# Four groups' weights held in a mixture of experts with capacity, and tokens gathered in three bf16 parts with one one-hot per pair of groups

## The reference, cut to what matters

```python
scores = jax.nn.softmax(x @ gate_w.T, axis=-1)
topk_w, topk_i = jax.lax.top_k(scores, K)
# pos: the place of a token in its expert's queue, in order of tokens
valid = pos < CAP
slot = jnp.where(valid, pos, CAP)
buf = jnp.zeros((E, CAP + 1, H), x.dtype).at[flat_i, slot].set(x[token_ids])
g = jnp.einsum('ech,ehi->eci', buf, w_gate)
u = jnp.einsum('ech,ehi->eci', buf, w_up)
y = jnp.einsum('eci,eih->ech', jax.nn.silu(g) * u, w_down)
out_slots = y[flat_i, slot] * (flat_w * valid)[:, None]
moe = out_slots.reshape(T, K, H).sum(axis=1)
shared = jax.nn.silu(x @ sw_gate) * (x @ sw_up) @ sw_down
```

## Time and profile before

| | us |
|---|---|
| median of 3 runs | 1891.27 |
| fastest, slowest of them | 1882.26, 1895.61 |
| profiled execution, its own time | 1897.17 |
| span of that execution | 1895.4 |

### The profile page before, as it was taken

One profiled execution on the slowest core, in us unless ns is written; L12 is line 12 of the kernel. 1 busy time (PEld: TensorE's weight loads), 2 busy tenths in 40 slices (PEclk: granted clock), 3 DMA queues, 4 the chain that ended last, 5 costly groups with the idle time before them and its releaser, 6 DMA issues.

```text
span 1895.4 us, 34583 instructions
## 1 busy us (share of the span) xinstructions
PE 1684.1 (89%) x10911; PEld 1349.1 (71%) x10912; DVE 1336.7 (71%) x2830; ACT 1020.7 (54%) x2200; POOL 659.1 (35%) x604
## 2 busy tenths in 40 slices
PE   3877999899999899989999998988799999988986
PEld 1224888677777888867777786756588888887664
DVE  7996777788884677777877656643788888656543
ACT  4665543578774554267777633111688888633111
POOL 1664410366661230046655422000455555321000
PEclk8998999899999899989999998988799999999989
DMA  1000210000000121000000012887011000012985
GB/s 62 0 1 25 84 51 1 15 20 19 19 6 35 42 76 43 1 23 18 24 20 11 15 47 62 257 228 203 26 31 33 25 25 17 30 44 87 255 222 148
DMA packets 34885, 111.36 MB, mean 59 GB/s; under 512 B 4992, under 2 KB 18544, under 8 KB 27888
## 3 DMA queue, kind: packets, MB, share of 16 engines
q1 hardware_dynamic: 34800, 110.26, 20.3%
HBM read 109.19 MB, written 1.05 MB: 58 GB/s over the span
## 4 chain that ended last, share of the span: by engine, by line
PE 57%; DVE 18%; DMA 10%; ACT 8%; issue 6%; ACTq 0%; DVEq 0%; POOL 0%; SPq 0%; POOLq 0%
DMA wgu<-in_w_gu 10%; PE banks L1033 7%; PE banks L1009 4%; PE banks L583 3%; PE banks L585 3%; PE banks L584 3%; PE banks L988 3%; PE banks L989 2%; PE banks L990 2%; ACT prob L1217 2%; PE banks L940 2%; PE banks L1047 2%; PE banks L942 2%; PE banks L941 2%; PE banks L1048 2%
## 5 line engine op out<-in xcount | busy, mean ns | idle before, releaser
L1457 POOL TENSOR_TENSOR xn<-xn 128x512 f32<-128x512 f32 x132 | 171.5, 1299 | 254.7 <-DVE xn L1341 254.7
L1443 POOL TENSOR_SCALAR prob<-prob,recip 128x256 f32<-128x256 f32 (+2 forms) x256 | 228.3, 907 | 68.1 <-DVE recip L1325 68.1
L1217 ACT ACTIVATE prob<-banks,peak 128x256 f32<-128x256 f32 (+3 forms) x384 | 190.3, 501 | 109.9 <-DVE peak L1316 99.9
L1033 PE MATMUL banks<-pt,v 128*128 128x256 f32 (+3 forms) x768 | 203.1, 407 | 7.2 <-ACT pt L1152 7.2
L1033 PEld LDWEIGHTS banks<-pt,v 128*128 128x128 f32 x768 | 143.6, 189 | 73.7 <-issue 32.9
L1316 DVE TENSOR_REDUCE peak<-banks 128x1 f32<-128x256 f32 (+3 forms) x384 | 161.3, 448 | 16.4 <-PE banks L992 15.4
L988 PE MATMUL banks<-k_hi,q_hi 128*128 128x256 f32 (+2 forms) x384 | 151.3, 394 | 24.1 <-DVE k_lo L1332 23.8
L1428 POOL TENSOR_TENSOR wq_lo<-wq,wq_hi 128x256 fp32r<-128x256 f32 x48 | 35.9, 748 | 343.2 <-ACT wq_hi L1167 343.2
L1009 PE MATMUL banks<-ident,prob 128*128 128x128 f32 x864 | 139.4, 277 | 3.2 <-DVE pt L1150 3.2
L1341 DVE TENSOR_TENSOR xn<-xn,ropes 128x512 f32<-128x512 f32 x138 | 122.4, 887 | 0.0
L681 POOL TENSOR_TENSOR w_parts<-raw,w_parts 128x768 fp32r<-128x768 f32 x36 | 67.3, 1870 | 157.3 <-ACT w_parts L637 157.3
(11 more groups left out here) (249 smaller groups left out, 5058.5 us busy)
## 6 DMA issues: line engine op xcount, KB each, us to landing
wgu<-in_w_gu SPq DMA_DIRECT2D x32, 1408.0 KB, 15.3
wd<-in_w_d SPq DMA_DIRECT2D x32, 704.0 KB
raw<-in_w SPq DMA_DIRECT2D x36, 384.0 KB, 3.1
wkv<-in_mha_kv SPq DMA_DIRECT2D x16, 256.0 KB, 2.7
wq<-in_mqa_q SPq DMA_DIRECT2D x16, 128.0 KB, 2.0
wo<-in_mqa_o SPq DMA_DIRECT2D x16, 128.0 KB, 2.1
wq<-in_gqa_q SPq DMA_DIRECT2D x16, 128.0 KB, 2.0
wo<-in_gqa_o SPq DMA_DIRECT2D x16, 128.0 KB, 2.1
```

Source lines behind the costliest of these rows:

```text
L1033: last = pe.matmul(o_bank[:, x * P:to], v[:, s, x, at:at + P], pt[:, s, x, first:first + to - x * P], start=(j == 0), stop=(j == NQ - 1))
L1217: last = act.activation(prob[:, s, cols[t]:cols[t] + n], s_bank[gi][:, psum_col[t]:psum_col[t] + n], ACT.Exp, bias=peak[:, s, t:t + 1], ac ...
L1443: last = pool.tensor_scalar(part, part, recip[:, s, t:t + 1], None, ALU.mult)
L1457: pool.tensor_tensor(cosed_at(i, m, r), cosed_at(i, m, r), swap[:, r % 2, :], ALU.add) \
```

## The change

- `wgu` and `wd` get four buffers each instead of two, so that the transfer for group n waits for group n-4. The loop's body is four groups long instead of two. The transfers of groups 0 and 1 are issued right behind those of the shared weights, before SP waits for `opened`; groups 2 and 3 behind it.
- To make room, `x_hi` and `x_lo` (fp32r) become `x_parts`, three parts in bf16. ACT makes the first, DVE takes it from `xn` in place, ACT makes the second, DVE the third. `gather` takes 48 matmuls instead of 32.
- `picks` and the buffer `pick` are gone. `pair` is bf16, has two buffers, and `weigh` and `spread` read the half of it that belongs to their group (`one_hot`). `spread` so waits for the pair (`paired`) where it waited for the group's own one-hot (`picked`).
- Other tiles move to other places in SBUF.

```diff
-    BODY = 2
+    BODY = 4
+    HALF = BODY // 2
...
+    wgu, wd = [], []
+    for area in (z3, z3, z1, z1):
+        wgu.append(area.take("wgu", [P, GE, NC, 2 * FF1], F32))
+        wd.append(area.take("wd", [HF1, GE, 2, H], F32))
...
+    x_parts = z1.take("x_parts", [P, 3, NT, H], BF16)
+    pair = pair_at.take("pair", [P, 2, NT, 2 * P], BF16)
...
+    def one_hot(m, t):
+        return pair[:, m // 2 % 2, t, m % 2 * P:(m % 2 + 1) * P]
...
+        def load(i, k):
+            at = bass.ds(BODY * i + k, 1) if not isinstance(i, int) else slice(BODY * i + k, BODY * i + k + 1)
+            wait(sp, c["inner"], k - BODY + 1, i, BODY)
+            sp.dma_start(wgu[k][:, :, :, :], d["w1_gu"][at].rearrange("o p e c n -> p (o e) c n")) \
+                .then_inc(gu_full[k].sem, 16)
+            wait(sp, c["down"], k - BODY + 1, i, BODY)
+            sp.dma_start(wd[k][:, :, :, :], d["w1_d"][at].rearrange("o p e c n -> p (o e) c n")) \
+                .then_inc(d_full[k].sem, 16)
+        load(0, 0)
+        load(0, 1)
         wait(sp, *opened)
         st.joined(sp)
+        load(0, 2)
+        load(0, 3)
+        with sp.Fori(1, NG1 // BODY) as i:
             for k in range(BODY):
+                load(i, k)
...
         def gather(i, q):
-            wait(pe, c["paired"], 2 * q + 2, i, 2)
-            wait(pe, c["buffered"], q, i, 1)
+            wait(pe, c["paired"], 2 * q + 2, i, BODY)
+            wait(pe, c["buffered"], q, i, HALF)
             for hc in range(NC):
                 for t in range(NT):
-                    for part in (x_hi, x_lo):
+                    for part in range(3):
...
         def spread(i, m, half):
             if half == 0:
-                wait(pe, c["picked"], m + 1, i, BODY)
+                wait(pe, c["paired"], 2 * (m // 2) + 2, i, BODY)
...
-                last = pe.matmul(b_spread[:, j * P:(j + 1) * P], pick[:, k, t, :], g.identb[:, :],
+                last = pe.matmul(b_spread[:, j * P:(j + 1) * P], one_hot(m, t), g.identb[:, :],
...
+        act.wait_ge(c["xrest"].sem, 1)
+        act.activation(x_parts[:, 1], g.xn[:, :, :], ACT.Copy).then_inc(c["xmiddle"].sem, 1)
...
+        dve.tensor_tensor(g.xn[:, :, :], g.xn[:, :, :], x_parts[:, 0], ALU.subtract).then_inc(c["xrest"].sem, 1)
...
-            if live(i, n + 2):
-                picks(i, n + 2)
...
         pairs(0, 0, 0)
         pairs(0, 0, 1)
-        picks(0, 0)
+        dve.wait_ge(c["xmiddle"].sem, 1)
+        dve.tensor_tensor(x_parts[:, 2], g.xn[:, :, :], x_parts[:, 1], ALU.subtract).then_inc(c["parted"].sem, 1)
```

More of the change, by code:

```diff
@@ L1514, in capacity_mixture @@
     sums = z3.take("sums", [P, NT], F32)
-    score = z3.take("score", [P, NT, NE1 + 2], F32)
-    left = z3.take("left", [P, NT, NE1 + 2], F32, top=True)
+    wtmp = z3.take("wtmp", [P, 2, GE * 3], F32)
+    wslot = z3.take("wslot", [P, 2], F32)
     top = z3.take("top", [P, NT, 8], F32)
@@ L1519, in capacity_mixture @@
     ahead = z3.take("ahead", [P, NT, NE1], BF16)
[L1520 to L1526, removed]
+    score = z1.take("score", [P, NT, NE1 + 2], F32)
+    left = z1.take("left", [P, NT, NE1 + 2], F32)
+    place = z1.take("place", [P, NT, NE1], F32)
+    wrest = z1.take("wrest", [P, NT, NE1], F32)
+    wpart = z1.take("wpart", [P, NT, NE1], BF16)
+    wparts = z1.take("wparts", [P, NT, NE1, 3], BF16)
+    x_parts = z1.take("x_parts", [P, 3, NT, H], BF16)
+    pair_at = Area(st.nc, st.g.xh_at, st.g.xh_at + 8192)
+    pair = pair_at.take("pair", [P, 2, NT, 2 * P], BF16)
+    shgu_lo = Area(st.nc, z4.low, z4.high).take("shgu_lo", [P, 2, NC, NSH * P], F32R)
+    shgu = z4.take("shgu", [P, 2, NC, NSH * P], F32)
+    shgu_hi = z4.take("shgu_hi", [P, 2, NC, NSH * P], F32R)
+    shd_lo = Area(st.nc, z4.low, z4.high).take("shd_lo", [P, NSH, H], F32R)
     shd = z4.take("shd", [P, NSH, H], F32)
-    shd_hi, shd_lo = (z3.take("shd", [P, NSH, H], F32R, top=True) for _ in range(2))
+    shd_hi = z4.take("shd_hi", [P, NSH, H], F32R)
+    z2_low = z2.low
     shsilu = z2.take("shsilu", [P, 2, SEQ], F32)
@@ L1532, in capacity_mixture @@
     shin_lo = z2.take("shin_lo", [P, NSH, T], F32R)
[L1533 to L1545, removed]
+    late_a, late_b = Area(st.nc, z2_low + 8192, z2_low + 16384), Area(st.nc, z2_low + 20480, z2_low + 32768)
+    buf = late_a.take("buf", [P, NC, 2 * P], F32)
+    silu = late_a.take("silu", [P, FF1], F32)
+    acted = late_a.take("acted", [P, FF1], F32)
+    actt = late_a.take("actt", [HF1, 2, P], F32)
+    y = late_a.take("y", [P, H], F32)
+    pickt = late_b.take("pickt", [P, 2, T], F32R)
+    yparts = late_b.take("yparts", [P, 2, 2, H], F32R)
     acc = g.banks[:, 0:4, :].rearrange("p a (b h) -> p (a b) h", b=2)
@@ L1655, in gather @@
         def gather(i, q):
-            wait(pe, c["paired"], 2 * q + 2, i, 2)
-            wait(pe, c["buffered"], q, i, 1)
+            wait(pe, c["paired"], 2 * q + 2, i, BODY)
+            wait(pe, c["buffered"], q, i, HALF)
             for hc in range(NC):
                 for t in range(NT):
-                    for part in (x_hi, x_lo):
-                        last = pe.matmul(b_gather[:, hc * 2 * P:(hc + 1) * 2 * P], part[:, t, hc * P:(hc + 1) * P],
-                                         pair[:, t, :], start=(t == 0 and part is x_hi),
-                                         stop=(t == NT - 1 and part is x_lo))
+                    for part in range(3):
+                        last = pe.matmul(b_gather[:, hc * 2 * P:(hc + 1) * 2 * P],
+                                         x_parts[:, part, t, hc * P:(hc + 1) * P], pair[:, q % 2, t, :],
+                                         start=(t == 0 and part == 0), stop=(t == NT - 1 and part == 2))
             last.then_inc(c["gathered"].sem, 1)
         def weigh(i, m):
-            k = m % 2
             wait(pe, c["sloted"], m, i, BODY)
@@ L1672, in weigh @@
             for t in range(NT):
-                last = pe.matmul(b_weight, pick[:, k, t, :], wparts_g[:, t, at, :].rearrange("p o w -> p (o w)"),
+                last = pe.matmul(b_weight, one_hot(m, t), wparts_g[:, t, at, :].rearrange("p o w -> p (o w)"),
                                  start=(t == 0), stop=(t == NT - 1))
@@ L1748, in _ @@
         slot(0, -1)
-        slot(0, 0)
-        slot(0, 1)
+        for n in range(BODY):
+            slot(0, n)
         with pe.Fori(1, LOOPS) as i:
@@ L1798, in slot @@
                 q = (n + 1) // 2
-                wait(act, c["gathered"], q + 1, i, 1)
+                wait(act, c["gathered"], q + 1, i, HALF)
                 wait(act, c["inner"], n + 1, i, BODY)
@@ L1842, in _ @@
     def _(dve):
-        for n in ("picked", "paired", "sloted", "kept0", "acted", "split"):
+        for n in ("paired", "sloted", "kept0", "acted", "split"):
             dve.sem_inc(c[n].sem, c[n].prime)
```

54 lines of the change are left out of this document (18 added, 36 removed).

## The result

| | median us | lowest to highest | runs |
|---|---|---|---|
| before | 1884.62 | 1867.63 to 1906.09 | 20 |
| after | 1891.08 | 1885.05 to 1897.73 | 20 |

The ratio of after to before is 1.0052, 95% interval 1.0028 to 1.0075: half a per cent slower, inside the 1% that the prediction called no change. The forecast was 1892 us. The profiled execution of after took 1889.22 us, 8.0 less than before's profiled one (1897.17) and 1.9 under its own median.

A forecast was written before the change was run, and what follows sets the result against it. Late weights cost the loops time, with PE's instruction list the next bound. Against the profiled 1897.17 us, -46.3 + 22.2 + 20.4 = -3.7 gave 1893.5 (1887.6 if runs differ elsewhere); forecast 1892 us, no change, range 1872 to 1912.

The forecast's parts named there:

- Waits for weights: Loops of both mixtures with capacity and the first's last slot: four buffers end all waits for weights, -46.3 us.
- The gather: PE's list, 16 gathers: 48 bf16 matmuls take 5.16 us instead of 3.77, +22.2 us, bounds +3 and +30.
- The new wait: PE's spread in 14 odd slots waits about 1.46 us for the second half of DVE's pair, +20.4 us.
- The one-hot and the opening: DVE drops 32 pick writes; an extra ACT copy and DVE subtraction open each mixture: cost 0, at most 1 us each.
- The pair: Two groups in the capacity loops: about 18.3 us (15.45 + 1.39 + 1.46), instead of 18.1 and 18.8.
- the sum: Whole kernel: -46.3 + 22.2 + 20.4 = -3.7 us against the profiled execution's 1897.17, giving 1893.5 us.
- The median: Whole kernel: 1893.5 us stands if before's runs differ in waits for weights; if elsewhere, 1887.6 us.
- A clock that falls in the new wait: PE in 14 odd slots: idling about 1.4 us lowers the clock, +18 to +26 us, 1910 to 1918; chance 0.14.
- A wait off the path: Spread in odd slots: DVE finishes the half earlier, so 14 x 1.46 us are not paid, 1872 us; chance 0.09.
- a cheap gather: PE's gathers: 19 us less at the lower bound (1873), 7.5 less at the skill's estimate (1884); chance 0.07 for both.
- Transfers that still bind: Capacity loops: transfers below 200 GB/s still set a pair's time, between 1890 and 1905 us; chance 0.08.

The follow-up runs named there:

- e5: Before, with the wgu transfer from the third group on bringing only two of four experts, the rest multiplied with old weights: 1851.14 us.
- e3: After, with four buffers kept but each weight transfer waiting for the group two back instead of four: 1889.76 us.
- e6: After, with the one-hot's second half written ahead of y and the gather over two parts instead of three, transfers four ahead: 1852.76 us.
- e1: After, with the second half of the pair's one-hot written ahead of y in the even slot: 1872.64 us.
- b2: Before, unchanged, profiled a second time in a single execution: 1878.26 us.
- e2: After, with the gather over two bf16 parts instead of three, the third part left out of the sum: 1863.83 us.
- e4: After, with the one-hot's second half written ahead of y and each transfer waiting for the group two back: 1877.97 us.

## Why the prediction was right

*Waits for weights, -46.3 us.* Right in size for the execution that it was read from (e5: -46.0). The two loops lost their waits, and the last slot of the first mixture went from 13.21 to 9.31 us. Not right was what I gave as the cause. I credited the four buffers, and called their failing the way in which transfers could still bind; e3 shows that at after's pace two groups of lead do as well. The prediction named both terms that lengthen the list and never put the longer pair into its own rate: it reckoned 200 GB/s for four buffers, but not 237 for two. The number came out because the longer list takes away all the waits, whatever the buffers do: it does not bear out the step that it was derived by. Four buffers alone, under a list of about before's length, do not end all the waits (e6).

*The gather, +22.2 us.* 5.25 - 3.77 = 1.48 us each, 23.7 for 16, against 1.39 and 22.2. The streaming row of the same type gave the pace within 2% (107.5 ns forecast, 109 measured). The Trainium skill (TensorE: Matmul & The Clock Gate, section Back-to-back issue gap) has 131 ns for 512 columns sustained, and the estimate from it was 98 for 256; neither the 215 of the earlier trace rows nor the 109 here agrees with it. The bounds of 83 and 118 ns held it.

*The new wait, +20.4 us.* 20.1 us in 14 waits are in the trace, and taking them away gave back 18.4 (e1), 1.32 us each. The order of DVE's list decided this, and the two rows that showed the half's end against spread's start were enough to foretell it.

*The one-hot and the opening, 0.* 32 writes fewer on DVE moved nothing: its busy time in a loop fell by 17 us and the loops did not follow. In the opening the new subtraction takes 2.28 us (2.38 reckoned) and spread starts right behind the shared expert's products, without a wait, in the second mixture as in the first:

```profile
1730.14 2.28 DVE L1987 TENSOR_TENSOR x_parts<-xn,x_parts 128x2048 bf16<-128x2048 f32 x1
...
1733.22 0.28 PE L1671 MATMUL banks<-shd_hi,shin_lo 128*128 128x256 f32 x1
1733.34 0.40 PE L1703 MATMUL banks<-identb,pair 128*128 128x128 bf16 x4
```

*The pair.* 18.3 us forecast, 18.22 and 18.24 measured.

*What was not foreseen.* The last slot of the second mixture took 10.75 us at clock 0.84, not 9, which is 1.8 more. And of the 8.0 us between the two profiled executions 4.5 lie in the second mixture without capacity, which the change does not touch: from its first product to the first of the attention behind it, 168.98 us in the first profile of before, 164.48 in after, 164.68 in b2. In the two stages that are changed, after is 3.9 and 0.5 us shorter: -4.3 in all, where the sum said -3.7. That they agree so closely is luck in part: from the first product of the second of these stages to the inner product of group 0, before's first profile took 46.95 us, b2 48.24, after 48.91 and e3 52.80, so this opening alone moves by more than the sum.

*The median.* The prediction left open whether the runs of before differ in their waits for weights, in which case 1893.5 stands whatever before's median is. They do, for the most part (b2, and the spreads). So after is 6.5 us over before's median and under its profiled time, with one and the same cause. The sum closes from the other side too: e5 has before's list without waits, 1851.14 us; the gathers add 23.7 and the new waits 18.4, together 1893.2, and after has 1891.08.

*The rivals.* A clock that falls in the new wait: both loops stand at 1.00, in spite of 14 idle stretches of 1.4 to 1.5 us. A wait off the path, and a cheap gather: e1 and e2 refute them. Transfers that still bind: not under this list, but they are close. With four ahead they show at 16.5 us a pair (e2) and at 15.2 (e6), not at 16.92 (e1); with two ahead at 16.92 (e4).

## What to carry to other kernels

Here deeper prefetch paid only where the engine's list for a step was shorter than that step's transfer at the rate that the trace shows, and then it gave a head start that is used up, not a faster rate; when an edit lengthens the list too, work that rate out again for the new length before giving the buffers any credit. When two producers are merged into one, look at what stands ahead of the merged one in its engine's in-order list: here the wait for another result, 1.32 us at 14 places, went away by moving one instruction ahead of it. A profiled execution of a kernel that waits for transfers is one draw from a wide spread, so a term read from it carries that spread with it.

## What the hardware showed unexpectedly

Idle time of the same length did not decide the clock. PE in the last slots of after: the first mixture, then the second, down product and the sum behind it.

```profile
1314.48 1.07 PE L1732 MATMUL banks<-wd,actt 88*32 88x256 f32 x16 [0.56 <-ACT actt L1825]
1317.00 2.17 PE L1744 MATMUL banks<-yparts,pickt 128*128 128x256 f32 x16 [1.45 <-DVE yparts L1979]
...
1876.04 1.07 PE L1732 MATMUL banks<-wd,actt 88*32 88x256 f32 x16 [0.56 <-ACT actt L1825]
1878.56 3.63 PE L1744 MATMUL banks<-yparts,pickt 128*128 128x256 f32 x16 [1.45 <-DVE yparts L1979]
```

The same instructions with the same idle times of 0.56 and 1.45 us ahead: sixteen matmuls took 2.17 us in the first mixture (granted clock 1.00 over that slot, the 2.4 GHz level) and 3.63 in the second (0.84 over the slot, so at the 1.2 GHz level in part). Nor is it the change or the waits for weights: without any such wait in the loop, the last slot of the second mixture took 9.28 us at 1.00 in e1, 10.63 at 0.84 in e3, and 10.58 at 0.84 in e5, which has before's list. What makes the difference no run here tells apart, and no experiment was made on it. The other surprise was the rate of the transfers: the first loop of the kernel before had 246 GB/s in one execution and 263 in another, and was 13 us shorter there. A mean rate is only the other side of a loop's length, but the single transfers took longer too: 15.3 us from issue to landing of `wgu` in the median over both mixtures of the first execution, 12.8 in the second. Why, no run here shows.
